# Adding the second bias of a graph layer behind the product instead of ahead of it

## What is computed

```python
norm = _cheb_norm(src, dst, x.shape[0])           # -dinv[src] * dinv[dst]
def cheb_conv(h, W0, W1, b):
    tx1 = segment_sum(h[src] * norm[:, None], dst)
    return h @ W0 + tx1 @ W1 + b
h = relu(layernorm(x))
h = layer_norm(cheb_conv(h, W1_0, W1_1, b1), gamma, beta)
h = where(h >= 0, h, 0.01 * h)
x = x + cheb_conv(h, W2_0, W2_1, b2)
```

## Time and profile before

| | |
|---|---|
| median of 3 runs | 2099.91 us (2099.4 to 2102.49) |
| profiled execution, its own time | 2099.47 us |
| span of its trace | 2097.6 us |
| PE busy | 1929.8 us (92%) |
| POOL busy | 1517.4 us (72%) |
| ACT busy | 1509.2 us (72%) |
| DVE busy | 1437.0 us (69%) |
| first line 1199 to the last | 1139.0 to 2085.4 us |
| first gather of line 589 to the last | 118.0 to 2078.1 us |

### The profile page before, as it was taken

How to read it: one execution, slowest core, us unless ns; L and a number is a source line. 1 busy time by engine, 2 the same in 40 slices (tenths; PEclk the granted TensorE clock), 3 DMA queues, 4 the chain that set the end, 5 groups by cost and what they waited for, 6 DMA issues and landing times.

```text
span 2097.6 us, 25858 instructions
## 1 busy us (share of the span) xinstructions
PE 1929.8 (92%) x6822; PEld 1075.0 (51%) x6822; DVE 1437.0 (69%) x3415; ACT 1509.2 (72%) x2715; POOL 1517.4 (72%) x1596
## 2 busy tenths in 40 slices
PE   3459999999999999999997999999999999999998
PEld 3445555555555555555554555555555554555555
DVE  9857777787777777778775655566555665555654
ACT  7837778887777787788875766676666676666665
POOL 2267777777777777777777777777777777777774
PEclk9769999999999999999998999999999999999999
DMA  9998888888888888888878888888888888888885
GB/s 252 272 269 271 237 242 241 241 241 241 238 239 240 240 238 240 241 241 240 241 217 264 252 252 253 253 243 253 252 255 253 250 246 250 254 252 247 248 249 169
DMA packets 187920, 514.94 MB, mean 245 GB/s; under 512 B 44460, under 2 KB 46147, under 8 KB 186528
## 3 DMA queue, kind: packets, MB, share of 16 engines
q0 software_dynamic: 128576, 422.78, 68.8%
q1 hardware_dynamic: 56374, 90.16, 12.5%
q10 hardware_dynamic: 2828, 0.42, 0.3%
HBM read 472.40 MB, written 40.84 MB: 245 GB/s over the span
## 4 chain that ended last, share of the span: by engine, by line
PE 53%; POOL 17%; DVE 14%; issue 9%; DMA 6%; ACT 1%; SPq 0%; DVEq 0%; ACTq 0%
PE ps L1304 26%; POOL arena L589 17%; PE ps L1492 11%; PE ps L1485 6%; DMA arena<-table,idx_all 5%; PE ps L1483 5%; DVE low L1092 3%; PE ps L1296 2%; DVE ps L1162 2%; DVE stats L1165 2%; DVE ps L1172 2%; DVE w_all L895 2%; PE ps L1417 1%; DVE work L895 1%; PE ps L1415 1%
## 5 line engine op out<-in xcount | busy, mean ns | idle before, releaser
L589 POOL DMA_INDIRECT arena<-table,idx_all x1536 | 1464.9, 954 | 478.8 <-issue 438.0
L1096 DVE TENSOR_TENSOR low<-arena,ps 128x512 fp32r<-128x512 f32 x517 | 350.0, 684 | 370.5 <-ACT ps L700 364.7
L1483 PE MATMUL ps<-high,hots 128*128 128x512 f32 x1034 | 582.2, 563 | 5.4 <-ACT high L700 4.5
L1492 PE MATMUL ps<-arena,hots_full 128*128 128x512 f32 x1060 | 540.5, 602 | 33.8 <-DMA arena<-table,idx_all 33.5
L700 ACT CAST ps<-arena 128x512 fp32r<-128x512 f32 x517 | 305.2, 590 | 279.0 <-DMA arena<-table,idx_all 255.6
L1485 PE MATMUL ps<-low,hots 128*128 128x512 f32 x1034 | 417.4, 404 | 21.6 <-DVE low L1092 21.6
L1092 DVE SCALAR_TENSOR_TENSOR low<-arena,ps 128x512 fp32r<-128x512 f32 x508 | 366.1, 742 | 60.6 <-ACT ps L699 56.1
L699 ACT ACTIVATE ps<-arena 128x512 fp32r<-128x512 f32 x508 | 348.9, 687 | 24.3 <-DMA arena<-table,idx_all 23.6
L699 ACT ACTIVATE high<-arena 128x512 fp32r<-128x512 f32 x508 | 362.0, 713 | 0.0
L700 ACT CAST high<-arena 128x512 fp32r<-128x512 f32 x517 | 318.6, 616 | 0.0
L1485 PEld LDWEIGHTS ps<-low,hots 128*128 128x128 f32 x1034 | 195.4, 189 | 181.0 <-issue 88.5
(11 more groups left out here) (172 smaller groups left out, 1444.6 us busy)
## 6 DMA issues: line engine op xcount, KB each, us to landing
arena<-table SPq DMA_DIRECT2D x106, 256.0 KB
arena<-table,idx_all POOLq DMA_INDIRECT x1550, 3.9
table<-arena SPq DMA_DIRECT2D x53, 256.0 KB, 4.0
arena<-in_x_dram SPq DMA_DIRECT2D x53, 256.0 KB, 5.2
out_dram<-arena SPq DMA_DIRECT2D x53, 256.0 KB, 4.5
table<-arena SPq DMA_DIRECT2D x10, 1124.4 KB
arena<-in_x_dram POOLq DMA_DIRECT2D x9, 1120.0 KB, 34.7
w_all<-in_L_gnn_W_dram SPq DMA_DIRECT2D x2, 1024.0 KB, 14.5
```

Of the source, the lines that this page charges most:

```text
L589: nc.gpsimd.indirect_dma_start(out=rows[u][0:rn, c, 0:RW if L == 0 else D], out_offset=None, in_=table[L][0:NEAR if near else N, :], in_of ...
L1096: nc.vector.tensor_tensor(low[a], rows[u][:, c, 0:D], high_ps[s % NB][:, :], ALU.subtract).then_inc(s_low, 1)
L1483: nc.tensor.matmul(tx_ps[u][:, :], hot, high[a], start=c == 0, stop=False)
L1492: last = nc.tensor.matmul(tx_ps[u][:, :], hot, rows[u][:, c, 0:D], start=c == 0, stop=i >= NC - 2 and c == SLOTS - 1)
```

## The change

In layer 2, chunks 0 to 51 no longer add the bias to the rows of x. `finish2` first multiplies the product bank by the scale and adds the rows of x, in place in the bank, and then adds the bias to the bank's content and writes `stage`. The second step waits for the first (`s_res`), for the table of layer 1 in chunk 0, and for the store of the chunk before (`s_out`). The last chunk keeps the two old steps under new names, `residual_last` and `finish_last`.

```diff
--- before.py
+++ after.py
@@ -1193,16 +1193,26 @@
                                                           in1=sloped[:, cols], op0=ALU.mult, op1=ALU.max)
                 last.then_inc(s_hs1, 1)
 
-            def residual2(i, u, h):
+            def finish2(i, u, h):
+                dve.wait_ge(s_d1, NC + i + 1)
+                dve.wait_ge(s_xr[u], 16 * (h + 1))
+                dve.sem_inc(s_dpass, 1)
+                nc.vector.scalar_tensor_tensor(out=mm_ps[u][:, :], in0=mm_ps[u][:, :], scalar=scale(i, 5),
+                                               in1=xin[u], op0=ALU.mult, op1=ALU.add).then_inc(s_res, 1)
+                if i == 0:
+
+                    dve.wait_ge(s_tab1, 16 * (NC + 1))
+                dve.wait_ge(s_res, i + 1)
+                dve.wait_ge(s_out, 16 * (i + 1))
+                nc.vector.tensor_tensor(stage, mm_ps[u][:, :], bias2, ALU.add).then_inc(s_fin, 1)
+
+            def residual_last(i, u, h):
 
                 dve.wait_ge(s_xr[u], 16 * (h + 1))
                 nc.vector.tensor_tensor(xin[u], xin[u], bias2, ALU.add).then_inc(s_res, 1)
 
-            def finish2(i, u):
+            def finish_last(i, u):
                 parts = products(i, u)
-                if i == 0:
-
-                    dve.wait_ge(s_tab1, 16 * (NC + 1))
                 dve.wait_ge(s_res, i + 1)
                 dve.wait_ge(s_out, 16 * (i + 1))
                 dve.sem_inc(s_dpass, 1)
@@ -1252,8 +1262,7 @@
                         if L == 0:
                             epi = conv_stats(i - 1, 1 - u)
                         else:
-                            residual2(i - 1, 1 - u, (i - 1) // 2)
-                            finish2(i - 1, 1 - u)
+                            finish2(i - 1, 1 - u, (i - 1) // 2)
                     lows(7, 8)
                     if L == 0 and i == 0:
                         count_second()
@@ -1279,8 +1288,8 @@
                     norm1(NC - 1, 0, conv_stats(NC - 1, 0))
                     finish1(NC - 1, 0)
                 else:
-                    residual2(NC - 1, 0, (NC - 1) // 2)
-                    finish2(NC - 1, 0)
+                    residual_last(NC - 1, 0, (NC - 1) // 2)
+                    finish_last(NC - 1, 0)
 
             with dve.If(bad > 0):
                 general(0)
```

## The result

| | before | changed |
|---|---|---|
| median of 7 runs | 2099.76 us (2096.03 to 2102.49) | 2092.82 us (2091.33 to 2093.88) |
| profiled execution | 2099.47 us | 2092.82 us |
| span of its trace | 2097.6 us | 2091.0 us |

The ratio is 0.9972, with a 95% interval of 0.9963 to 0.9982. The change makes the kernel 7 us faster, a third of a per cent. The forecast of 2093.8 us was 1.0 us too high, and the range held the time.

The account below looks back on a forecast made before the run. GpSimd's gathers, one after another, were taken to set the pace; fifteen held by the old addition in layer 2 gave 5.7 us, the new pair and the end cost 0: 2099.47 - 5.7 = 2093.8 us, range 2091.0 to 2097.5.

Follow-up runs that it names:

- k3: The kernel before, with its layer-2 addition of bias2 to the rows of x moved behind the wait for the product: 2100.43 us against 2102.53 before, ratio 0.9995.
- e4: The kernel before, its layer-2 bias2 addition moved behind the wait for the product, on a slow chip: 2488.54 us against 2476.04 before, ratio 1.0032.
- f2: The kernel before, its bias2 addition moved behind the wait for the product, as e4 but on another slow chip: 2489.02 us against 2482.45, ratio 1.0038.
- e2: The changed kernel plus one unused SBUF addition per layer-2 chunk, ahead of the product wait, slow chip: 2486.53 us against 2476.04 for the kernel before, ratio 1.0039.
- e5: The changed kernel plus two unused SBUF additions back to back per layer-2 chunk, slow chip: 2486.26 us against 2476.04 for the kernel before, ratio 1.0046.

## What to carry to other kernels

Where one queue sets the pace and its gap is constant, look for its instructions that are longer than the median and list what the other engines began just before them; their excess, one by one, is the price of the neighbour, and the neighbour's form can be changed (here, one input in PSUM) at a cost that an engine with slack bears. Work that is put behind a wait costs nothing as long as the engine behind it has idle time to give; whether that is so is read from the waits of the queue that sets the pace, on the chip on which the kernel is to run. And cut a trace at the same few instructions before and after: two terms of 3 us that cancel are not seen in the total.

## What was not expected of the hardware

**The exclusion works both ways.** In k3 at 1468.73 us the addition begins 0.02 us ahead of the gather. The gather takes its usual 0.95 us, and the addition 0.74 us instead of 0.69. Of e4 one such place:

```profile
1353.24 0.75 DVE L1201 TENSOR_TENSOR arena<-arena 128x512 f32<-128x512 f32 x1 [9.27 <-remote]
1353.27 0.94 POOL L589 DMA_INDIRECT arena<-table,idx_all  x1 [2.82 <-remote]
```

There are thirteen such places (one in k3, eight in e4, four in f2), with the gather's start 0.02 to 0.04 us behind the addition's, and in all it is the addition that is longer, 0.74 or 0.75 us. In the other order it is seen too: before, the three additions that begin 0.01 to 0.03 us behind a gather take 0.70 to 0.71 us, the others 0.67 to 0.69. The border isn't a matter of that offset alone, since before three gathers, one 0.01 and two 0.05 us behind, are held (1.49 and 1.45 us), and in e2 one that is recorded 3 ns ahead of the addition (1.51 us); there the addition waits for nothing, in the thirteen places it comes out of a wait. Which of the two matters is open. (The expectation of f2 counts seven of e4's eight.)

Where a gather is held, its length and its offset add up to 1.50 us: 0.01 + 1.49, 0.28 + 1.22 before, 0.13 + 1.39 in k3. It goes on 0.55 us into the addition, whenever it began. That fits something which both need, the addition for its first 0.55 us and the gather at its beginning only, and it would be why a gather 0.6 us into the addition is free. What that thing is, the traces don't say; they show the times alone.

Every profile has another such pair, once, in layer 1, at a longer instruction with both inputs in SBUF, line 1031 (bf16, 1.09 us). In e5:

```profile
162.26 1.09 DVE L1031 TENSOR_TENSOR work<-counts,ids_near 128x1792 bf16<-128x1792 bf16 x1 [2.15 <-PE ps L1412]
162.41 1.76 POOL L589 DMA_INDIRECT arena<-table,idx_all  x1 [0.30 <-issue]
```

Here the gather goes on 0.96 us into the instruction (0.15 + 1.76 - 0.95), and so within 0.01 us in all fourteen profiles, with offsets of 0.15 to 0.90 us. Like the 0.55 us of the addition of 0.68 us, that is 0.13 us before the end. So the hold isn't bound to float32 or to this addition, and it grows with the length of the instruction.

**A gather can be held through two additions.** In e5 at two of them back to back:

```profile
1553.70 0.69 DVE L1198 TENSOR_TENSOR work<-arena 128x512 f32<-128x512 f32 x1
1553.78 2.03 POOL L589 DMA_INDIRECT arena<-table,idx_all  x1 [0.30 <-issue]
1554.31 0.69 DVE L1199 TENSOR_TENSOR work<-arena 128x512 f32<-128x512 f32 x1
```

It takes 2.03 us, that is 1.08 us over the usual. The second addition begins 0.61 us behind the first, so it leaves no gap to slip into, and 37 of the 40 gathers that began inside such a pair were stretched, where before a single addition stretched 15 of 25.

**One program, two paces.** The kernel before takes 2098 to 2103 us on some chips and 2476 to 2514 us on others. An experiment on a few tenths of a per cent means little until its time before is compared with the one that the question is about.
